# Causal attention in an eight-core transformer layer: both heads of a pair in one pass over the keys instead of one head after the other

## The chip, the cores and the metric

The kernel runs on all 8 cores of one Trainium2 chip (trn2). Each core computes one batch element and none talks to another. The metric is the device time in microseconds of the slowest core.

## The reference

One layer, post-norm, on x of shape (8, 2048, 1024), f32. The change touches the attention only.

```python
q = (x @ Wq + bq).reshape(b, s, 16, 64)      # k and v the same way
q = _apply_rope(q, sin, cos); k = _apply_rope(k, sin, cos)
scores = jnp.einsum('bqhd,bkhd->bhqk', q, k) * scale
scores = scores + jnp.where(causal, 0.0, -10000.0)
attn = jax.nn.softmax(scores, axis=-1)
ctx = jnp.einsum('bhqk,bkhd->bqhd', attn, v).reshape(b, s, 1024)
x = _layernorm(x + ctx @ Wo + bo)
# router: softmax, top 2 of 8 experts
# out = shared expert + sum over 8 experts of w[e] * expert(e), each computed densely
x = _layernorm(x + out)
```

## The kernel before

The program is written out by hand: every engine gets its instructions in the order of the code, and waits on semaphores are placed by `Ring` (buffers used in turn) and `Prog.wait`. VectorE (DVE), ScalarE (ACT) and GpSimd (POOL) also wait, before each operation, for their own previous one (`Prog.op`, `SELF_FENCE`).

The stages on a core are these. First x is transposed to xbf and v is computed for all heads. Then comes attention, which is the function shown below. Then the output projection with the layer norm and the router, then nine experts (the shared one and eight), each with 4096 hidden units, then the last layer norm. The experts' weights come as f32 and are converted to bf16 by DMAs from HBM to HBM (`precast_expert`: four DMAs of 4096 KB per expert). They are issued on POOL's queue, experts 0 and 1 at the start, expert j + 2 in attention pair j.

Attention works on 8 pairs of heads (j). For each pair:

- POOL issues the loads of wq and wk (256 KB each, two buffers each), then the conversion of expert j + 2. PE waits for both loads.
- PE projects q and k for both heads of the pair (L354, 64 matmuls, 128x128 weights), ACT moves them to SBUF with the bias (L363), PE permutes them (L372), DVE multiplies with the sine table (L379), POOL multiplies with the cosine table and adds (L388, L393). Head A stands on partitions 0 to 63 of qr_sb and kr_sb, head B on 64 to 127.
- Then, head after head, four windows of 512 queries. A window has 4, 8, 12 or 16 key tiles of 128 keys, since later keys are masked; the last four of a window carry the causal mask. For each key tile PE computes the scores into a buffer of pS (L467, or L455 and L460, where the mask is added by a matmul with the identity), ACT takes the exponential into et (L472), and one tile later PE adds the values (L405, into pCt) and the sum of the exponentials (L409, a matmul with a column of ones, into pSm). Two pS and three et buffers are in use.
- At the end of a window DVE copies the sums to SBUF (L488) and takes the reciprocal (L491, one partition, 512 elements). At the fourth key tile of the next window PE spreads it over 128 partitions (L419, f32, which runs as two matmul instructions), DVE copies that to SBUF (L425) and multiplies it with the values (L431).

The next pair's first operation on qr_sb waits for the scores of this pair, so the loads for pair j + 1 are issued on POOL right behind the rope of pair j.

Of the kernel before, what the change touches and what calls it, by code (L numbers as in the profile page):

```python
# [8 lines left out]
F32 = mybir.dt.float32  # L9
# [5 lines left out]
S = 2048  # L15
# [119 lines left out]
def build_nc():  # L135
# [20 lines left out]
    din("sel8", [8, 1024], BF16)  # L156
    y = nc.dram_tensor("y", [S, D], F32, kind="ExternalOutput").ap()
# [26 lines left out]
    sel8 = E(nc.sbuf_tensor("sel8_s", [8, 1024], BF16))  # L184

# [19 lines left out]
    for name, dst in (("identf", identf), ("ropec", ropec), ("ropes", ropes),  # L205
                      ("prm", prm), ("identb", identb), ("trit", trit),
                      ("bqr", bq_sb), ("bkr", bk_sb), ("bor", bo_sb),
                      ("br1r", br1_sb), ("br2", br2row), ("bv", bvrow),
                      ("sel8", sel8)):
        p.dma("sync", dst[:, :], d[name], dC)  # L210
# [91 lines left out]
    with ExitStack() as ph:  # L302
# [7 lines left out]
        et_sb = [ph.enter_context(nc.sbuf_tensor(f"et{i}", [128, 512], BF16)) for i in range(3)]  # L310
# [3 lines left out]
        pS = [ph.enter_context(nc.psum_tensor(f"pS{i}", [128, 512], F32)) for i in range(2)]  # L314
        pCt = [ph.enter_context(nc.psum_tensor(f"pCt{i}", [128, 512], F32)) for i in range(3)]
        pSm = [ph.enter_context(nc.psum_tensor(f"pSm{i}", [1, 512], F32)) for i in range(2)]
        pMs = ph.enter_context(nc.psum_tensor("pMs", [128, 512], F32))

        for eng in ("tensor", "scalar", "vector", "gpsimd"):
            p.wait(eng, dC, consts_d)  # L320

# [8 lines left out]
        pms_free = 0  # L330
        recip_free = 0
# [3 lines left out]
        for j in range(NCH):  # L335
# [61 lines left out]

            def emit_av(pa):
                p.wait("tensor", tA, pa["ex"])
                p.op("tensor",  # L400
                     lambda e, o=pa["ctslot"][pa["r0"]:pa["r0"] + 64, :],
                     l=vbuf[:, pa["kt"] * D + pa["h"] * 64: pa["kt"] * D + pa["h"] * 64 + 64],
                     r=pa["ets"][:, :], st=(pa["kt"] == 0), sp=(pa["kt"] == pa["nkt"] - 1),
                     tp=(0, pa["r0"]):
                     e.matmul(o, l, r, start=st, stop=sp, tile_position=tp))  # L405
                sm = p.op("tensor",
                          lambda e, o=pa["smslot"][:, :], r=pa["ets"][:, :],
                          st=(pa["kt"] == 0), sp=(pa["kt"] == pa["nkt"] - 1):
                          e.matmul(o, ones_b[:, :], r, start=st, stop=sp),  # L409
                          inc=tT)  # L410
                et_ring.release(pa["eti"], tT, sm)
                return sm

            def emit_norm(pn):
                nonlocal recip_free, pms_free
                p.wait("tensor", tV, pn["rc"])
                p.wait("tensor", tV, pms_free)
                bt = p.op("tensor", lambda e:
                          e.matmul(pMs[:, :], ones_f[:, :], recip_sb[0:1, :],  # L419
                                   start=True, stop=True), inc=tT)  # L420
                recip_free = bt
                rslot, rbi = rb_ring.acquire("vector")
                p.wait("vector", tT, bt)
                bv_ = p.op("vector", lambda e, o=rslot[:, :]:
                           e.tensor_copy(o, pMs[:, :]), inc=tV)  # L425
                pms_free = bv_
                r0_, j_, win0_ = pn["r0"], pn["j"], pn["win0"]
                cv = p.op("vector",
                          lambda e, o=ctx[r0_:r0_ + 64, j_ * S + win0_: j_ * S + win0_ + 512],
                          i=pn["ctslot"][r0_:r0_ + 64, :], r=rslot[r0_:r0_ + 64, :]:  # L430
# [6 lines left out]
            for hh in range(2):  # L437
                h = 2 * j + hh
                r0 = 64 * hh
                for qh in range(2):  # L440
                    for ws in range(2):
                        win0 = qh * 1024 + ws * 512
                        nkt = qh * 8 + ws * 4 + 4
                        ctslot, cti = ct_ring.acquire("tensor")
                        smslot, smi = sm_ring.acquire("tensor")
                        for kt in range(nkt):
                            sslot, ssi = ps_ring.acquire("tensor")
                            ets, eti = et_ring.acquire("scalar")
                            off = kt * 128 - win0
                            if off >= 0:  # L450
                                p.op("tensor",
                                     lambda e, o=sslot[:, :],
                                     l=kr_sb[r0:r0 + 64, kt * 128:(kt + 1) * 128],
                                     r=qr_sb[r0:r0 + 64, win0:win0 + 512]:
                                     e.matmul(o, l, r, start=True, stop=False))  # L455
                                scol = 384 - off
                                st_t = p.op("tensor",
                                            lambda e, o=sslot[:, :],
                                            m=trit[:, scol:scol + 512]:
                                            e.matmul(o, identb[:, :], m, start=False,  # L460
                                                     stop=True), inc=tT)
                            else:
                                st_t = p.op("tensor",
                                            lambda e, o=sslot[:, :],
                                            l=kr_sb[r0:r0 + 64, kt * 128:(kt + 1) * 128],
                                            r=qr_sb[r0:r0 + 64, win0:win0 + 512]:
                                            e.matmul(o, l, r, start=True, stop=True),  # L467
                                            inc=tT)
                            p.wait("scalar", tT, st_t)
                            ex = p.op("scalar",  # L470
                                      lambda e, o=ets[:, :], i=sslot[:, :]:
                                      e.activation(out=o, in_=i, func=AF.Exp,  # L472
                                                   bias=cst[:, 0:1], scale=cst[:, 1:2]),
                                      inc=tA)
                            ps_ring.release(ssi, tA, ex)
                            if kt == 3 and pend_norm is not None:
                                emit_norm(pend_norm)
                                pend_norm = None
                            if pend_av is not None:
                                emit_av(pend_av)  # L480
# [581 lines left out]
```

How the kernel before makes its waits and increments, by code:

```python
    def wait(self, eng, sem, val):  # L43
        if val <= 0:
            return
        if sem == self.SELF_FENCE.get(eng):
            if self._lastwait.get(eng, 0) >= val:
                return
            self._lastwait[eng] = val
        h = self.sems[sem]
        self.q[eng].append(lambda e, h=h, v=val: e.wait_ge(h, v))
# [1 line left out]
    def op(self, eng, build, inc=None, n=1):  # L53
        own = self.SELF_FENCE.get(eng)
        if own is not None:
            self.wait(eng, own, self.cnt[own])
            if inc is None:
                inc, n = own, 1
        if inc is None:
            self.q[eng].append(build)
            return None
        self.cnt[inc] += n
        h = self.sems[inc]
        self.q[eng].append(lambda e, b=build, h=h, k=n: b(e).then_inc(h, k))
        return self.cnt[inc]
# [1 line left out]
    def dma(self, eng, out, in_, sem):  # L67
        self.cnt[sem] += 16
        h = self.sems[sem]
        self.q[eng].append(lambda e, o=out, i=in_, h=h: e.dma_start(out=o, in_=i).then_inc(h, 16))
        return self.cnt[sem]
```

## Time and profile before

| | us |
|---|---|
| median of 3 runs | 6456.24 |
| all runs | 6455.94, 6456.24, 6901.99 |
| profiled execution | 6476.09 |
| its span, slowest core (3) | 6474.3 |
| spans of the 8 cores | 6447.9 to 6474.3 |
| attention stage in it (first projection to first load of the next stage) | 444.5 to 2064.6 |

The profile is that of core 3. Its spans are from the first to the last instruction; PE is TensorE's matmul, PEld its weight load, which can lie beside a matmul. PEclk is the clock that TensorE was granted, as a share of 2.4 GHz. The ends of matmuls are modelled and overlap the next one's start, so distances between starts are the better measure of what one costs.

### The profile page before, as it was taken

To read this page: it belongs to the slowest core of one execution; us is meant where nothing else is said; L and a number is where in the kernel's file an instruction comes from. 1 tells how busy PE (TensorE), PEld (TensorE's weight loads), DVE (VectorE), ACT (ScalarE), POOL (GpSimd) and SP (SyncE) were. 2 spreads that over 40 slices of the span, in tenths; PEclk is the share of its full clock that TensorE was granted. 3 is DMA by queue.
4 is the path that set the end of the run, shared out by engine and by line. 5 is a ranking of instruction groups with operands and counts; after the bars stand their busy time and mean duration, and the time that the engine had idled before them with its cause. 6 is when DMAs were issued, how large, how long until landed. Compare 5 with 4: busy or idle time off the path is not lost. (4 is left out here: it accounts for less than half of the span.)

```text
span 6474.3 us, 62496 instructions; the slowest of 8 cores (6447.9 to 6474.3 us)
## 1 busy us (share of the span) xinstructions
PE 5732.0 (89%) x22486; PEld 2264.1 (35%) x22486; DVE 987.7 (15%) x1255; ACT 1488.4 (23%) x2064; POOL 834.8 (13%) x717
## 2 busy tenths in 40 slices
PE   0069988899888589999999999999999999999996
PEld 0031111111111334444444444444444444444443
DVE  0012222222222401100100110111011001001104
ACT  0013333333333431122122112212211221221122
POOL 0010111101110000001211221121022012112211
PEclk9995555555555789999999999999999999999996
DMA  9949998788101110101010010101010010101101
GB/s 127 119 77 112 112 112 94 82 98 91 20 1 17 52 40 33 46 33 46 27 53 27 33 46 33 46 27 53 27 44 35 33 46 27 53 27 39 40 33 59
DMA packets 40060, 342.76 MB, mean 53 GB/s; under 512 B 5579, under 2 KB 5963, under 8 KB 16468
## 3 DMA queue, kind: packets, MB, share of 16 engines
q0 software_dynamic: 10368, 159.92, 21.7%
q1 hardware_dynamic: 29396, 178.85, 7.5%
q8 instruction: 191, 3.13, 0.2%
q14 instruction: 105, 0.86, 0.1%
HBM read 490.27 MB, written 159.38 MB: 100 GB/s over the span
## 5 line engine op out<-in xcount | busy, mean ns | idle before, releaser
L879 PE MATMUL pE<-h1bf,w2s 128*128 128x512 bf16 x9216 | 2010.4, 381 | 20.0 <-ACT h1bf L861 20.0
L850 PE MATMUL pE<-x2bf,w1s 128*128 128x512 bf16 x9216 | 2011.1, 381 | 6.9 <-DMA w1s<-w1bf 6.9
L861 ACT ACTIVATE h1bf<-pE,b_sb 128x512 bf16<-128x512 f32 x1152 | 791.7, 687 | 3155.7 <-PE pE L850 3155.5
L879 PEld LDWEIGHTS pE<-h1bf,w2s 128*128 128x128 bf16 x9216 | 904.7, 98 | 1125.6 <-issue 88.5
L850 PEld LDWEIGHTS pE<-x2bf,w1s 128*128 128x128 bf16 x9216 | 905.6, 98 | 1109.7 <-issue 35.4
L911 POOL TENSOR_TENSOR x<-x,tmp 128x512 f32<-128x512 f32 x512 | 647.9, 1266 | 3491.9 <-DVE tmp L902 3491.9
L472 ACT ACTIVATE et<-pS,cst 128x512 bf16<-128x512 f32 x640 | 497.7, 778 | 886.5 <-PE pS L460 455.3
L902 DVE SCALAR_TENSOR_TENSOR tmp<-pE,b_sb,wb 128x512 f32<-128x512 f32 x256 | 192.1, 751 | 1604.8 <-PE pE L879 1604.8
L405 PE MATMUL pCt<-et,vbuf 128*64 128x512 bf16 x640 | 401.9, 628 | 32.0 <-ACT et L472 32.0
L902 DVE SCALAR_TENSOR_TENSOR tmp<-pE,wb 128x512 f32<-128x512 f32 x256 | 177.0, 691 | 1620.5 <-PE pE L879 1620.5
L409 PE MATMUL pSm<-et,ones_b 128*1 128x512 bf16 x640 | 373.6, 584 | 0.0
L245 PE MATMUL pX<-identf_s,xstage 128*128 128x128 f32 x128 | 30.8, 423 | 342.4 <-DMA xstage<-x 341.0
L467 PE MATMUL pS<-qr_sb,kr_sb 64*128 64x512 bf16 x384 | 223.1, 606 | 0.0
L405 PEld LDWEIGHTS pCt<-et,vbuf 128*64 128x64 bf16 x640 | 81.4, 127 | 395.1 <-issue 395.1
L491 DVE RECIPROCAL recip_sb<-sums_sb 1x512 f32<-1x512 f32 x64 | 213.8, 3341 | 6.6
L455 PE MATMUL pS<-qr_sb,kr_sb 64*128 64x512 bf16 x256 | 154.2, 602 | 61.9 <-POOL kr_sb L393 61.9
L388 POOL TENSOR_TENSOR qr_sb<-q_sb,ropec_s 128x512 bf16<-128x512 bf16 x32 | 37.1, 1160 | 1225.9 <-ACT q_sb L363 1222.4
L488 DVE COPY sums_sb<-pSm 1x512 f32<-1x512 f32 x64 | 43.4, 679 | 873.1 <-PE pSm L409 872.1
L419 PE MATMUL pMs<-recip_sb,ones_f 1*128 1x512 f32 x128 | 132.2, 1134 | 36.4 <-DVE recip_sb L491 36.4
L460 PE MATMUL pS<-trit_s,identb_s 128*128 128x512 bf16 x256 | 155.9, 609 | 0.0
L409 PEld LDWEIGHTS pSm<-et,ones_b 128*1 128x1 bf16 x640 | 50.6, 79 | 279.3 <-issue 279.3
L245 PEld LDWEIGHTS pX<-identf_s,xstage 128*128 128x128 f32 x128 | 25.2, 223 | 347.5 <-issue 347.5
(121 smaller groups left out, 1400.0 us busy)
## 6 DMA issues: line engine op xcount, KB each, us to landing
w1bf<-w1r POOLq DMA_DIRECT2D x18, 4096.0 KB, 119.7
w2bf<-w2r POOLq DMA_DIRECT2D x18, 4096.0 KB, 154.6
w1s<-w1bf SPq DMA_DIRECT2D x72, 1024.0 KB, 7.2
w2s<-w2bf SPq DMA_DIRECT2D x72, 1024.0 KB, 7.7
xstage<-x SPq DMA_DIRECT2D x16, 512.0 KB, 4.4
xres<-x SPq DMA_DIRECT2D x16, 512.0 KB, 3.3
y<-ybuf SPq DMA_DIRECT2D x16, 512.0 KB, 2.6
wv_sb<-wv POOLq DMA_DIRECT2D x8, 256.0 KB, 16.3
```

The lines of the kernel that those rows point to most:

```text
L405: e.matmul(o, l, r, start=st, stop=sp, tile_position=tp))
L409: e.matmul(o, ones_b[:, :], r, start=st, stop=sp),
L455: e.matmul(o, l, r, start=True, stop=False))
L460: e.matmul(o, identb[:, :], m, start=False, stop=True), inc=tT)
L467: e.matmul(o, l, r, start=True, stop=True),
L472: e.activation(out=o, in_=i, func=AF.Exp, bias=cst[:, 0:1], scale=cst[:, 1:2]),
L491: rc = p.op("vector", lambda e: e.reciprocal(recip_sb[:, :], sums_sb[:, :]), inc=tV)
L850: e.matmul(o, l, r, start=st, stop=sp),
L861: e.activation(out=o, in_=i, func=AF.Silu, bias=b), inc=tA)
L879: e.matmul(o, l, r, start=st, stop=sp),
L902: e.scalar_tensor_tensor(o, i, b, w, ALU.add, ALU.mult),
L911: e.tensor_tensor(o, o, t, ALU.add), inc=tG)
```

## The change

Both heads of a pair are handled in the same pass over the key tiles. Per key tile PE computes the scores of head A and of head B into two pS buffers, ACT takes two exponentials, and one tile later PE does value A, value B, sum A, sum B. Head A's values go to the array's columns 0 to 63 and to partitions 0 to 63 of one pCt buffer, head B's to columns and partitions 64 to 127 (`tile_position`). The sums go to partitions 0 and 64 of one pSm buffer. The scores contract over rows 0 to 63 for A and 64 to 127 for B, as they did before. There are four windows per pair instead of eight, with twice the work in each.

The buffers change from two to four pS, from three to four et, and from three to two pCt; pMs goes, and pSm grows to 128 partitions. The copy to sums_sb goes: DVE takes two reciprocals, straight from pSm, on partitions 0 and 64. The broadcast is a matmul of a new constant sel2 (65 x 128) with recip_sb (65 x 512, set to 1 once), written into the same pSm buffer. ACT waits once per key tile, for the last of the score and mask matmuls, and signals once, after the second exponential.

```diff
-        et_sb = [... (f"et{i}", [128, 512], BF16)) for i in range(3)]
-        sums_sb = ph.enter_context(nc.sbuf_tensor("sums_sb", [1, 512], F32))
-        recip_sb = ph.enter_context(nc.sbuf_tensor("recip_sb", [1, 512], F32))
+        et_sb = [... (f"et{i}", [128, 512], BF16)) for i in range(4)]
+        recip_sb = ph.enter_context(nc.sbuf_tensor("recip_sb", [65, 512], F32))
-        pS = [... [128, 512] ... for i in range(2)]
-        pCt = [... [128, 512] ... for i in range(3)]
-        pSm = [... [1, 512] ... for i in range(2)]
-        pMs = ph.enter_context(nc.psum_tensor("pMs", [128, 512], F32))
+        pS = [... [128, 512] ... for i in range(4)]
+        pCt = [... [128, 512] ... for i in range(2)]
+        pSm = [... [128, 512] ... for i in range(2)]
...
             def emit_av(pa):
                 p.wait("tensor", tA, pa["ex"])
-                p.op("tensor", ... e.matmul(ctslot[r0:r0+64], vbuf[h], ets, tile_position=(0, r0)))
-                sm = p.op("tensor", ... e.matmul(smslot[:, :], ones_b, ets), inc=tT)
+                p.op("tensor", ... e.matmul(ctslot[0:64], vbuf[hA], etsA, tile_position=(0, 0)))
+                p.op("tensor", ... e.matmul(ctslot[64:128], vbuf[hB], etsB, tile_position=(0, 64)))
+                p.op("tensor", ... e.matmul(smslot[0:1], ones_b, etsA))
+                sm = p.op("tensor", ... e.matmul(smslot[64:65], ones_b, etsB, tile_position=(0, 64)), inc=tT)
...
             def emit_norm(pn):
-                bt = p.op("tensor", ... e.matmul(pMs[:, :], ones_f[:, :], recip_sb[0:1, :]), inc=tT)
+                bt = p.op("tensor", ... e.matmul(smslot, sel2[0:65, 0:128], recip_sb[0:65, :]), inc=tT)
...
-            for hh in range(2):
-                for qh in range(2):
-                    for ws in range(2):
+            for qh in range(2):
+                for ws in range(2):
...
+                        for (r0, sslot) in ((0, sslotA), (64, sslotB)):
+                            last = (off < 0) and (r0 == 64)
+                            p.op("tensor", ... e.matmul(sslot, kr_sb[r0:r0+64, kt], qr_sb[r0:r0+64, win0], stop=sp),
+                                 inc=(tT if last else None))
+                        if off >= 0:
+                            for sslot in (sslotA, sslotB):
+                                p.op("tensor", ... e.matmul(sslot, identb, trit[scol:scol+512], start=False, stop=True),
+                                     inc=(tT if sslot is sslotB else None))
+                        p.wait("scalar", tT, st_t)
+                        p.op("scalar", ... Exp, etsA <- sslotA)
+                        ex = p.op("scalar", ... Exp, etsB <- sslotB, inc=tA)
...
                     sm = emit_av(pend_av)
                     p.wait("vector", tT, sm)
-                        sc = p.op("vector", ... e.tensor_copy(sums_sb[:, :], smslot))
-                        rc = p.op("vector", ... e.reciprocal(recip_sb[:, :], sums_sb[:, :]), inc=tV)
+                    p.op("vector", ... e.reciprocal(recip_sb[0:1, :], smslot[0:1, :]), inc=tV)
+                    rc = p.op("vector", ... e.reciprocal(recip_sb[64:65, :], smslot[64:65, :]), inc=tV)
```

On PE, in the first window of pair 0 (all key tiles masked), the order before was this (pS score, pCt values, pSm sums; the number behind a name is its buffer):

```order
L455 MATMUL pS0<-qr_sb,kr_sb 128x512
L460 MATMUL pS0<-trit_s,identb_s 128x512
L455 MATMUL pS1<-qr_sb,kr_sb 128x512
L460 MATMUL pS1<-trit_s,identb_s 128x512
L405 MATMUL pCt0<-et0,vbuf 64x512
L409 MATMUL pSm0<-et0,ones_b 1x512
L455 MATMUL pS0<-qr_sb,kr_sb 128x512
L460 MATMUL pS0<-trit_s,identb_s 128x512
```

And in the same place now:

```order
L473 MATMUL pS0<-qr_sb,kr_sb 128x512
L473 MATMUL pS1<-qr_sb,kr_sb 128x512
L480 MATMUL pS0<-trit_s,identb_s 128x512
L480 MATMUL pS1<-trit_s,identb_s 128x512
L473 MATMUL pS2<-qr_sb,kr_sb 128x512
L473 MATMUL pS3<-qr_sb,kr_sb 128x512
L480 MATMUL pS2<-trit_s,identb_s 128x512
L480 MATMUL pS3<-trit_s,identb_s 128x512
L408 MATMUL pCt0<-et0,vbuf 64x512
L414 MATMUL pCt0<-et1,vbuf 64x512
L418 MATMUL pSm0<-et0,ones_b 1x512
L423 MATMUL pSm0<-et1,ones_b 1x512
```

Matmuls of one shape now stand in twos, the first for head A and the second for head B.

On PE, the passage from the first to the second window of a head, before, up to the broadcast of the reciprocal:

```order
L467 MATMUL pS0<-qr_sb,kr_sb 128x512
L467 MATMUL pS1<-qr_sb,kr_sb 128x512
L405 MATMUL pCt1<-et1,vbuf 64x512
L409 MATMUL pSm1<-et1,ones_b 1x512
L467 MATMUL pS0<-qr_sb,kr_sb 128x512
L405 MATMUL pCt1<-et2,vbuf 64x512
L409 MATMUL pSm1<-et2,ones_b 1x512
L467 MATMUL pS1<-qr_sb,kr_sb 128x512
L419 MATMUL pMs<-recip_sb,ones_f 128x512
```

And now:

```order
L408 MATMUL pCt1<-et2,vbuf 64x512
L414 MATMUL pCt1<-et3,vbuf 64x512
L418 MATMUL pSm1<-et2,ones_b 1x512
L423 MATMUL pSm1<-et3,ones_b 1x512
L473 MATMUL pS2<-qr_sb,kr_sb 128x512
L473 MATMUL pS3<-qr_sb,kr_sb 128x512
L434 MATMUL pSm0<-recip_sb,sel2_s 128x512
L408 MATMUL pCt1<-et0,vbuf 64x512
L414 MATMUL pCt1<-et1,vbuf 64x512
```

The broadcast still stands behind the fourth key tile's scores, and now writes the previous window's pSm buffer.

## Rows read from the trace of the kernel before

**Rows 1.** The page: the span in 40 slices, clock and DMA.
```profile
PEclk9995555555555789999999999999999999999996
DMA  9949998788101110101010010101010010101101
```

**Rows 2.** Stretches: length, PE busy and instructions, further engines where shown, clock, DMA share, GB/s.
```profile
677.50:849.00 171.50, 162.49 (x289) 0.50 1.01 113
...
850.00:880.00 30.00, 17.47 (x71) 6.85 (x69) 6.19 (x9) 5.50 (x8) 19.29 (x18) 0.84 0.98 108
```

**Rows 3.** Groups by line in the attention stage, 480 to 2064 us.
```profile
L472 ACT ACTIVATE et<-pS,cst 128x512 bf16<-128x512 f32 x638 | 496.1, 778 | 875.2 <-PE pS L460 444.1 <-PE pS L467 426.1 <-ACT et L472 0.7
...
L467 PE MATMUL pS<-qr_sb,kr_sb 64*128 64x512 bf16 x384 | 223.1, 606 | 0.0
L491 DVE RECIPROCAL recip_sb<-sums_sb 1x512 f32<-1x512 f32 x64 | 213.8, 3341 | 6.6
```

**Rows 4.** Timeline from 927 us: start us, length us, engine, line, operation.
```profile
927.49 0.61 PE L460 MATMUL pS<-trit_s,identb_s 128*128 128x512 bf16 x1
928.02 0.63 PE L405 MATMUL pCt<-et,vbuf 128*64 128x512 bf16 x1
...
930.22 1.03 PE L467 MATMUL pS<-qr_sb,kr_sb 64*128 64x512 bf16 x2
...
930.98 1.65 ACT L472 ACTIVATE et<-pS,cst 128x512 bf16<-128x512 f32 x2 [1.96 <-PE pS L467]
...
932.44 0.58 PE L409 MATMUL pSm<-et,ones_b 128*1 128x512 bf16 x1
932.96 0.60 PE L467 MATMUL pS<-qr_sb,kr_sb 64*128 64x512 bf16 x1
933.49 0.63 PE L405 MATMUL pCt<-et,vbuf 128*64 128x512 bf16 x1
...
934.05 0.58 PE L409 MATMUL pSm<-et,ones_b 128*1 128x512 bf16 x1
```

**Rows 5.** Timeline at the boundaries of pairs 1 and 2, and of 6 and 7.
```profile
842.58 0.68 DVE L488 COPY sums_sb<-pSm 1x512 f32<-1x512 f32 x1 [22.23 <-PE pSm L409]
...
846.95 2.04 PE L419 MATMUL pMs<-recip_sb,ones_f 1*128 1x512 f32 x2 [4.55 <-DVE recip_sb L491]
848.92 8.60 PE L354 MATMUL pS<-xbf,wq 128*128 128x512 bf16 x32
...
879.70 0.58 PE L455 MATMUL pS<-qr_sb,kr_sb 64*128 64x512 bf16 x1 [7.75 <-POOL kr_sb L393]
...
1859.34 1.03 PE L354 MATMUL pS<-xbf,wq 128*128 128x512 bf16 x2
```

**Rows 6.** Timeline: issues of wk by POOL; DMA issues: us to landing, last.
```profile
444.46 1.86 PE L354 MATMUL pS<-xbf,wq 128*128 128x512 bf16 x4 [9.49 <-DMA wk<-wkr]
...
476.48 0.55 POOL L70 DMA_DIRECT2D wk<-wkr  x1
...
wk<-wkr POOLq DMA_DIRECT2D x1, 256.0 KB, 122.9
...
678.13 0.55 POOL L70 DMA_DIRECT2D wk<-wkr  x1
...
wk<-wkr POOLq DMA_DIRECT2D x1, 256.0 KB, 77.7
...
879.79 0.55 POOL L70 DMA_DIRECT2D wk<-wkr  x1
...
wk<-wkr POOLq DMA_DIRECT2D x1, 256.0 KB, 31.4
...
wk<-wkr POOLq DMA_DIRECT2D x1, 256.0 KB, 7.1
```

**Rows 7.** Timeline: the first load of the stage behind attention.
```profile
2064.59 4.30 POOL L70 DMA_DIRECT2D wo_sb<-wor  x8 [173.73 <-POOLq L79]
```

**Rows 8.** Stretch behind the last conversion, columns as the second of rows 2.
```profile
1640.00:1660.00 20.00, 15.45 (x30) 3.62 (x30) 5.41 (x4) 3.58 (x5) 0.00 (x0) 0.50 0.00 0
```

More of the change, by code:

```diff
@@ L156, in build_nc @@
     din("sel8", [8, 1024], BF16)
+    din("sel2", [65, 128])
     y = nc.dram_tensor("y", [S, D], F32, kind="ExternalOutput").ap()
@@ L410, in emit_av @@
                           inc=tT)
-                et_ring.release(pa["eti"], tT, sm)
+                et_ring.release(pa["etiA"], tT, sm)
+                et_ring.release(pa["etiB"], tT, sm)
                 return sm
             def emit_norm(pn):
-                nonlocal recip_free, pms_free
+                nonlocal recip_busy
                 p.wait("tensor", tV, pn["rc"])
[L417 to L420, printed above, removed]
@@ L421, in emit_norm @@
-                recip_free = bt
+                bt = p.op("tensor", lambda e, o=pn["smslot"][:, :]:
+                          e.matmul(o, sel2[0:65, 0:128], recip_sb[0:65, :],
+                                   start=True, stop=True, skip_group_check=True),
+                          inc=tT)
+                recip_busy = bt
                 rslot, rbi = rb_ring.acquire("vector")
                 p.wait("vector", tT, bt)
-                bv_ = p.op("vector", lambda e, o=rslot[:, :]:
-                           e.tensor_copy(o, pMs[:, :]), inc=tV)
@@ L436, in build_nc @@
             pend_norm = None
-            for hh in range(2):
-                h = 2 * j + hh
-                r0 = 64 * hh
-                for qh in range(2):
-                    for ws in range(2):
[L442 to L450, printed above, removed]
-                                p.op("tensor",
[L452 to L480, printed above, removed]
-                            pend_av = dict(ex=ex, ctslot=ctslot, smslot=smslot,
-                                           kt=kt, nkt=nkt, ets=ets, eti=eti,
-                                           h=h, r0=r0)
-                        sm = emit_av(pend_av)
-                        pend_av = None
-                        p.wait("vector", tT, sm)
-                        sc = p.op("vector", lambda e, i=smslot[:, :]:
-                                  e.tensor_copy(sums_sb[:, :], i), inc=tV)
-                        sm_ring.release(smi, tV, sc)
-                        p.wait("vector", tT, recip_free)
-                        rc = p.op("vector", lambda e: e.reciprocal(recip_sb[:, :], sums_sb[:, :]),
-                                  inc=tV)
-                        pend_norm = dict(rc=rc, ctslot=ctslot, cti=cti,
-                                         r0=r0, j=j, win0=win0)
```

110 lines of the change are left out of this document (91 added, 19 removed).

## The prediction

> **What bounds the kernel now.** I read the page's forty slices first [rows 1]. Slices 3 to 12 are the attention stage: there the clock granted to PE reads 5 (half speed, the 1.2 GHz level) where the later stages read 9, and the DMA row is nearly full beside it. The change touches only this stage, 444.5 to 2064.6 us, so the rest of the span should stay as it is.
>
> Next, the stage by stretches [rows 2]: between 677.5 and 849 us PE is busy 162.5 of 171.5 us at clock 0.50, so PE ends the waits here. The DMA share in the same row is 1.01. The groups and the timeline [rows 3, 4] say what fills PE: matmuls that use half of the array's rows (64x128 scores), half of its columns (128x64 values) or one column (128x1 sums), and the full 128x128 mask. By [rows 3] ACT's exps are busy 496 of 1584 us, and DVE takes 64 reciprocals on one partition, 3.34 us each.
>
> The timeline [rows 4] gives the step that counts (durations overlap, so I take start to start): mask 0.53, value 0.56, sum 0.52, score 0.53 us. Two score matmuls of the same kind in a row last 1.03 together against 0.60 for one, so the second costs 0.43 (= 512 columns at 1.2 GHz); a matmul that follows one of another shape costs 0.10 more. One key tile of one head costs 1.61 us (value 0.56, sum 0.52, score 0.53), and 2.15 with the mask.
>
> Last, the boundary of two head pairs [rows 5] and the weight loads [rows 6]. A pair's pitch is (1859.34 - 848.92)/5 = 202.1 us. It checks: projections and rope 30.8 (848.92 to 879.70), 80 key tiles (48 x 1.61 + 32 x 2.15 = 146.1), 8 broadcasts of the reciprocal at 2.04 = 16.3, the wait for the last reciprocal 4.6: 197.8, and some 4 at the joins of the windows.
>
> **The queue behind the loads.** [Rows 6] decide the size of the gain. POOL issues a pair's wq and wk just after the rope of the pair before, behind a 16 MB conversion of expert weights. wk of pair 1 is issued at 476.48 and lands 122.9 later, at 599.4; of pair 2 at 678.13 + 77.7 = 755.8; of pair 3 at 879.79 + 31.4 = 911.2; of pair 4 in 7.1. Small loads of equal size do not take 122.9 and 7.1 by themselves: they wait in turn behind the conversions. Landings follow each other by 156.4 and 155.4, and the first (pair 0, 444.46, where PE waited for it) fits with 154.9; the mean is 155.6 us per expert. Now a pair takes 202, so the queue empties and nobody waits. A pair shorter than 155.6 will wait for its weights, each time.
>
> **The change part by part.**
>
> *Two heads in one pass.* The number of score, value, sum and mask matmuls stays the same. What changes is their order: always two of one shape in a row, on two disjoint halves of the array: score on rows 0 and 64, value on columns 0 and 64, sum the same. So of six changes of shape per key tile of a pair three remain, and eight become four with the mask.
>
> *The price x of the second matmul of such a two.* No row of before shows two different tiles one after the other. Upper bound: 0.43, the second of equal shape in [rows 4]. Lower bound: 0, if it runs beside the first; they share no cell, no PSUM partition (value, sum) or bank (scores), and read different operands. Below nothing is excluded, since the first one stands. I take x = 0, on the ground that none of the rows shows a common resource that is full, and keep 0.43. What makes this choice less bold: the result hardly depends on x until the pair's pitch exceeds 155.6 (below). The Trainium skill (TensorE: Matmul & The Clock Gate, Part 3) says that matmuls on different tiles run concurrently and gives 2.38x for three column tiles; no row here shows it. By that figure three matmuls cost 1.26 of one, an estimate of x = 0.13 x 0.43 = 0.06; with it the pair would cost 7 more and the kernel, which waits for its loads anyway, 6076.
>
> *With x = 0:* PE needs 1.61 per pair of unmasked tiles; with the mask 2.15 plus a second mask matmul of the same shape and weights, 0.43: 2.58.
>
> *ACT.* Two exps in a row take 1.65 [rows 4], 0.87 from start to start, so 1.74 per two. Scores go two tiles ahead (four pS). The loop is exp(k), then value and sum(k), then score(k+2), then exp(k+2): 1.65 + 1.61 + 0.35 for two hand-overs between engines ([rows 5]: copy at 842.58, 0.68 + 3.34 later 846.60, norm at 846.95), over two tiles: 1.8. With the mask PE's 2.58 is longer, so 2.6: 24 x 1.8 + 16 x 2.6 = 84.8.
>
> *Reciprocals.* Still 3.34 each, but two in a row (partitions 0 and 64) per window, 6.9 with the hand-over; from PSUM rather than SBUF, whose price no row shows: [rows 5] has DVE's copy out of PSUM at 0.68, and the SBUF reciprocal takes 3.34, so between none and +0.7 each; I take none. The copy into sums goes (0.68). In all 64 reciprocals as before, but PE's norm matmul at the fourth tile now meets a later one. PE has by then done 4 scores and 2 value-sum pairs, held back by exps; it reaches the norm some 4.5 us after the first exp, the reciprocals are ready about 6.4 after it. With the 2.04 of the norm, value, sum and score of the next tile behind it, ACT stands still for about 3.2. The join itself (value and sum, then score, after the last exp) is some 1.9: 5 x 3 joins = 15.
>
> *End of a pair.* Value and sum 1.1, two reciprocals 6.9, norm 2.04, hand-overs 0.3: 10.3, before the next projection. Norms: four of 2.04 instead of eight; K = 65 instead of 1, for which [rows 3, 4] show no dependence (score with 64 rows 0.606, mask with 128 rows 0.61).
>
> *Projection and rope*, 30.8: POOL's chain of 16 operations holds it (PE idles 7.75 for kr at its end [rows 5]). Four pS instead of two free PE earlier, nothing more. The new constant (33 KB), the memset of recip_sb and its wait come once: nothing.
>
> *Sum.* Pair: 30.8 + 84.8 + 15 + 10.3 = 140.9. That is below 155.6, so from pair 1 on PE waits for wk: 14.7 us per pair. Pair 7 starts at 444.46 + 7 x 155.6 = 1533.7. In before its projection starts at 1859.34 and the next stage's first load is issued at 2064.59 [rows 5, 7], 205.3 later; now 205.3 - (202.1 - 140.9) = 144.1 later, at 1677.8. The gain is 386.8. Had the loads not been in the way, it would be 8 x 61.2 = 490. The profiled execution is 6476.1 (span 6474.3): it becomes 6089; against the median, 6456.2, 6069.
>
> The conversions end at about 1534 instead of 1640 (behind it the DMA share is 0.00 [rows 8]), before the stage in which they are read; nothing collides there.
>
> **The clock.** In [rows 2] it is 0.50 while PE is busy 95%, and it is 0.84 in the projection between 850 and 880, where PE is less busy but the matmuls are full 128x128: what PE did before the clock fell was narrow matmuls. The two-head order lays two halves side by side, so it might rise. The Trainium skill (TensorE: Matmul & The Clock Gate, Part 1) says that a PE kept busy is given the full clock. By that rule, which gives rival 1, the clock of [rows 2] could not be 0.50; the trace contradicts it as far as busy time goes.
>
> **Rivals.**
> 1. *The clock rises inside attention.* For: full-width work has 0.84 and more. Against: exps leave PE idle in part. Then ACT sets all tiles: 40 x 1.74 = 69.6, joins 11, end of pair 8.7, rope 30.8: 120. The start of pair 7 stays; only 21 less at its end: 6048.
> 2. *The second matmul does not run beside the first* (x = 0.43). Then a pair costs per tile 3 x 0.97 = 2.9, with mask 3.86: 24 x 2.9 + 16 x 3.86 = 131.4, rope 30.8, norms inside 6.1, end 10 (reciprocals hidden inside): 178. Gain 8 x 24 = 193: 6263. The change would then not do its main work, only save changes of shape.
> 3. *Half of it*: rows pack, columns do not, or x about 0.3: pitch 158 to 165, PE-bound again, gain 8 x (202.1 - 161) = 329: 6127.
> 4. *Slower.* Alternating tiles drain PE fully: each matmul then costs its weight load and its own length, 0.10 + 0.61 = 0.71 [rows 3]: 24 x 6 x 0.71 + 16 x 8 x 0.71 = 193, with 47 for the rest 240: 8 x 38 = 304 slower, 6760. It turns at a mean step of (202.1 - 47)/272 = 0.57. Against: equal shapes follow each other at 0.43 today.
> 5. *No turn in the queue*: pairs start when ready, 490 gained, 5966. [Rows 6] speak against it.
>
> **How the numbers follow.** Forecast (packed, clock as now) 0.45; rival 1 0.32; rival 3 0.07; rival 2 0.10; rival 4 0.03; rival 5 0.03. The first two share the term that decides, 1533.7, and differ by what one pair costs, 120 to 155: 6048 to 6084, a few us more for the pitch (7 x 1). The range takes them and rival 3: 6030 to 6165. A measurement of this kernel tells about 2% from no change, 129 us; every case but the fourth gains more, so faster 0.95, same 0.02, slower 0.03.
>
> **What would show it.** Right: PE idle 10 to 35 us before the first wq matmul of pairs 1 to 7, released by the wk load; these starts 155.6 apart; second scores starting under 0.15 after the first; one DMA stretch at share 1.0 from 0.44 to 1.53 ms; PE waiting for recip_sb about 2 us in each window. Wrong: starts more than 156 apart with no wait for wk (packing fails, see the step from one half to the other), or wk landing early while conversions run.

## The result and the profile after

The changed kernel takes 6076.74 us (median of all its runs). In some executions of either kernel the cores of one die run at a lower granted clock, so times are compared from here on by the other executions alone: 6066.3 to 6083.4 us for the changed kernel, median 6071.5, and a ratio to the kernel before of 0.9406, 95% interval 0.9393 to 0.9419. The forecast was 6069, its range 6030 to 6165.

The profiled execution took 6068.34, its slowest core is core 0, span 6066.7 us. On that same core the next stage's first load, which ends attention, is issued at 1672.80, against 2075.13 on core 0 of before (2064.59 on core 3, [rows 7]). What follows that issue takes 4394 us on core 0, against 4387 before. So the gain lies in attention alone.

The page's forty slices, to be read against [rows 1]:

```profile
PE   0065566666656999999999999999999999999996
...
PEclk9996666666677999999999999999999999999997
DMA  9949999999021100100100101101001001001001
```

The stage has shrunk to slices 3 to 10. The clock there reads 6 instead of 5, PE is no longer full, and DMA is full to the end of slice 9. PE is not the bound any more. Who is, the waits of PE from 440 to 1690 us say (engine, tile and line, released by: us in total, times, longest):

```profile
PE pS L354 <- DMA wk<-wkr: 161.6, 8, 24.5
PE pCt L408 <- ACT et L491: 122.4, 183, 1.7
PE pSm L434 <- DVE recip_sb L511: 93.4, 32, 7.6
PE pS L473 <- POOL kr_sb L393: 91.1, 8, 11.6
```

The first line is the wait that the forecast named: eight waits, the first of 9.5 as in [rows 6], seven of 16 to 24.5. The timeline shows where they stand and how far apart (start, length, operation, idle time before it and its releaser):

```profile
447.10 9.65 PE L354 MATMUL pS<-xbf,wq 128*128 128x512 bf16 x32 [9.50 <-DMA wk<-wkr]
...
602.77 2.72 PE L354 MATMUL pS<-xbf,wq 128*128 128x512 bf16 x6 [21.12 <-DMA wk<-wkr]
...
758.50 6.67 PE L354 MATMUL pS<-xbf,wq 128*128 128x512 bf16 x20 [24.48 <-DMA wk<-wkr]
...
1536.42 9.42 PE L354 MATMUL pS<-xbf,wq 128*128 128x512 bf16 x32 [16.48 <-DMA wk<-wkr]
...
1672.80 2.71 POOL L70 DMA_DIRECT2D wo_sb<-wor  x5 [106.27 <-POOLq L79]
```

(1536.42 - 602.77)/6 = 155.6 us: the pitch of the landings in [rows 6], to a tenth; over the eight cores it is 155.1 to 155.8. wk of pair 1 is issued at 478.00 and lands 124.5 later, wk of pair 7 at 1416.35 and lands 119.8 later; in before the fourth and later ones took 7.1 or less, because the queue had run empty.

The key tiles look like this (start, length), at the beginning of pair 0:

```profile
481.33 0.61 PE L408 MATMUL pCt<-et,vbuf 128*64 128x512 bf16 x1 [0.44 <-ACT et L491]
481.33 0.63 PE L414 MATMUL pCt<-et,vbuf 128*64 128x512 bf16 x1
481.89 0.59 PE L418 MATMUL pSm<-et,ones_b 128*1 128x512 bf16 x1
481.90 0.59 PE L423 MATMUL pSm<-et,ones_b 128*1 128x512 bf16 x1
482.42 0.61 PE L473 MATMUL pS<-qr_sb,kr_sb 64*128 64x512 bf16 x2
482.96 1.04 PE L480 MATMUL pS<-trit_s,identb_s 128*128 128x512 bf16 x2
...
486.52 0.40 PE L408 MATMUL pCt<-et,vbuf 128*64 128x512 bf16 x1
486.52 0.40 PE L414 MATMUL pCt<-et,vbuf 128*64 128x512 bf16 x1
```

Value A and value B start at the same time, the sums 0.01 apart, and the two scores last 0.61 together, as long as one did. Only the masks, which share the whole array, follow each other (1.04). The steps from one shape to the next are those of before: 0.56, 0.52, 0.54. The Trainium skill (TensorE: Matmul & The Clock Gate, Part 3) gives about 4 ns between the starts of matmuls on different tiles; the trace, with 0.00 to 0.01 us, agrees. From 486.52 on the lengths are 0.40 instead of 0.61: here the clock is at its upper level, 2.4 GHz.

By stretches (columns as in [rows 2]), a whole pair with its wait:

```profile
602.00:757.00 155.00, 93.56 (x352) 24.38 (x352) 37.87 (x24) 67.69 (x88) 21.72 (x22) 0.65 1.00 112
```

The DMA share is 1.00 and PE is busy 94 of 155 us. [Rows 2] had 162.5 of 171.5 without the projection.

Inside a pair the clock goes up and down. Near the end of the second window of pair 1, where the key tiles carry the mask, it is at its upper level; behind it, at the lower one again (columns as above):

```profile
657.50:663.50 6.00, 4.53 (x26) 1.27 (x24) 0.31 (x1) 4.15 (x7) 0.00 (x0) 1.00 1.13 127
664.50:680.50 16.00, 13.19 (x42) 2.77 (x43) 6.77 (x4) 10.94 (x15) 0.00 (x0) 0.50 0.92 102
```

From score to score, over all eight pairs of core 0 and without the joins of the windows, an unmasked key tile of a pair takes 1.83 us and a masked one 2.19.

### The profile page after: what moved, and what is told of

Same layout as the page of the kernel before. It is cut to its first block and busy times, and to the rows that moved or that the text cites. A ratio compares the mean times of both kernels' runs of the same rounds, so it can differ in the third digit from the quotient of the medians.

```text
span 6066.7 us, 61212 instructions; the slowest of 8 cores (6054.4 to 6066.7 us)
## 1 busy us (share of the span) xinstructions
PE 5020.7 (83%) x22422; PEld 2146.7 (35%) x22422; DVE 901.4 (15%) x1128; ACT 1488.5 (25%) x2064; POOL 835.9 (14%) x717
## 5 line engine op out<-in xcount | busy, mean ns | idle before, releaser
L408 PE MATMUL pCt<-et,vbuf 128*64 128x512 bf16 x320 | 165.7, 518 | 124.4 <-ACT et L491 122.4
L473 PE MATMUL pS<-qr_sb,kr_sb 64*128 64x512 bf16 x640 | 162.8, 517 | 91.1 <-POOL kr_sb L393 91.1
L354 PE MATMUL pS<-xbf,wq 128*128 128x512 bf16 x256 | 75.8, 469 | 161.6 <-DMA wk<-wkr 161.6
L509 DVE RECIPROCAL recip_sb<-pSm 1x512 f32<-1x512 f32 x32 | 107.1, 3346 | 536.3 <-PE pSm L423 526.2
L414 PE MATMUL pCt<-et,vbuf 128*64 128x512 bf16 x320 | 171.7, 537 | 0.0
L423 PE MATMUL pSm<-et,ones_b 128*1 128x512 bf16 x320 | 159.0, 497 | 0.0
L418 PE MATMUL pSm<-et,ones_b 128*1 128x512 bf16 x320 | 158.4, 495 | 0.0
L408 PEld LDWEIGHTS pCt<-et,vbuf 128*64 128x64 bf16 x320 | 37.9, 119 | 306.6 <-issue 306.6
L434 PE MATMUL pSm<-recip_sb,sel_s 65*128 65x512 f32 x64 | 65.4, 1126 | 93.4 <-DVE recip_sb L511 93.4
```

Source lines behind the costliest of these rows:

```text
L408: e.matmul(o, l, r, start=st, stop=sp, tile_position=(0, 0), skip_group_check=True))
L414: e.matmul(o, l, r, start=st, stop=sp, tile_position=(0, 64), skip_group_check=True))
L418: st=first: e.matmul(o, ones_b[:, :], r, start=st, stop=False, skip_group_check=True))
L423: e.matmul(o, ones_b[:, :], r, start=st, stop=sp, tile_position=(0, 64), skip_group_check=True),
L473: e.matmul(o, l, r, start=True, stop=sp),
```

## The experiments

"Pitch" is the mean distance between the starts of pairs 1 to 7, on the slowest core unless cores are named. The runs were spread over several chips.

### Who sets the pace: weight loads ahead of the conversions

```diff
-        wq_sb = [... for i in range(2)]      # wk_sb the same
+        wq_sb = [... for i in range(8)]
-        for j in range(NCH):
-            wqs, wqi, qtok = wq_ring.load("gpsimd", ...)
-            wks, wki, ktok = wk_ring.load("gpsimd", ...)
+        for j in range(NCH):
+            wload.append(wq_ring.load("gpsimd", ...) + wk_ring.load("gpsimd", ...))
+        for j in range(NCH):
+            wqs, wqi, qtok, wks, wki, ktok = wload[j]
```

The same edit was made to the changed kernel and to the kernel before.

> The changed kernel, with eight wq and eight wk buffers and all sixteen loads issued ahead of the conversions of experts 2 to 8. Theory (the pairs wait for wk because it stands behind a conversion in POOL's queue): the waits of PE for wk, 161.6 us in the changed kernel, fall to the first one of some 10; pairs start 131 to 134 apart instead of 155.6; the kernel is 152 us faster than the changed one, 5915 to 5930. Rival (the conversions take the DMA engines' bandwidth, and whoever loads has to wait until they are done): no gain, 6060 to 6080, pitch 156.

Measured: 5937 to 5942 us, some 132 less than the changed kernel. PE waits for wk once, 8.7 us, at the first pair; pitch 133.1. The conversions still run at share 1.00, so it is the place in the queue and not the bandwidth that held the pairs. The gain is 20 short of what was expected, on which more below.

> The kernel before, with the same eight buffers and early loads. Theory: nothing waits for wk there, pitch 202, so no difference (within 8 us of before, ratio 0.999 to 1.001). Rival (early loads help in themselves): a gain like that of the loads in the changed kernel, 100 us or more.

Measured: 6456.5 to 6458.1, the kernel before 6457.0 to 6457.7 beside it. No difference. The queue only costs something once a pair is shorter than a conversion.

### Where the shorter pairs come from: the order on PE

First the twos were taken apart, the other parts of the change kept (score B and its mask stand behind value A and sum A). One more thing moved: the broadcast of the reciprocal now stands before the fourth key tile's scores instead of behind them.

```diff
-                        for (r0, sslot) in ((0, sslotA), (64, sslotB)):
-                            p.op("tensor", ... score)          # A, B
-                        ... mask A, mask B
-                            emit_av(pend_av)                   # value A, value B, sum A, sum B
+                        for (r0, sslot) in ((0, sslotA), (64, sslotB)):
+                            if r0 == 64 and pend_av is not None:
+                                emit_av_a(pend_av)             # value A, sum A
+                            p.op("tensor", ... score); ... mask
+                        ... exponentials
+                            emit_av_b(pend_av)                 # value B, sum B
```

> The changed kernel with all its buffers, two-head pass, half as many norms and signals, but PE's order is score A, (mask A), value A, sum A, score B, (mask B), value B, sum B, so that no two neighbours have one shape except at the start of a window. Theory (the gain comes from equal shapes on two tiles standing side by side): 24 x 3.22 + 16 x 4.3 = 146 for the key tiles, with 31 rope, 8 norms, some 11 for the end and the joins: pitch 195 to 198, clock 0.50, no wait for wk, 6400 to 6430, ratio to before 0.991 to 0.996. Rival (the gain comes from larger buffers, fewer norms and fewer hand-overs): pitch under 175, under 6250.

Measured: 6485.3 to 6485.9, slower than before by 28 us and 56 over the upper end of the expectation. Pitch 204.9, clock 0.50 in the key tiles. The timeline (start, length) tells why. The score here is score B, L499 is the exponential of head A and L503 that of head B:

```profile
704.00 0.61 PE L408 MATMUL pCt<-et,vbuf 128*64 128x512 bf16 x1 [1.53 <-ACT et L503]
...
705.05 0.60 PE L486 MATMUL pS<-qr_sb,kr_sb 64*128 64x512 bf16 x1
...
705.81 0.78 ACT L499 ACTIVATE et<-pS,cst 128x512 bf16<-128x512 f32 x1 [1.96 <-PE pS L486]
...
706.68 0.78 ACT L503 ACTIVATE et<-pS,cst 128x512 bf16<-128x512 f32 x1
...
707.60 0.60 PE L408 MATMUL pCt<-et,vbuf 128*64 128x512 bf16 x1 [0.33 <-ACT et L503]
```

A key tile of a pair takes 3.60, not 3.22. ACT waits for the second score before it starts the first exponential, and PE for the second exponential before value A: with score B late in the tile, value A, sum A, score B and both exponentials form a chain. That was a flaw of the experiment, and it was mended with a wait and a signal for each head:

```diff
-                        p.wait("scalar", tT, st_t)
-                        p.op("scalar", ... Exp, etsA)
+                        p.wait("scalar", tT, st_a)
+                        exa = p.op("scalar", ... Exp, etsA)
+                        p.wait("scalar", tT, st_t)
...
-                p.wait("tensor", tA, pa["ex"])                 # before value A
+                p.wait("tensor", tA, pa["exa"])
```

> As the run with the twos apart, but with one signal and one wait for each score and each exponential, since there ACT waited for both scores and PE for both exponentials (a key tile cost 3.60 instead of 3.22 us). Theory: PE then runs without these waits at the steps of the kernel before, pitch 195 to 198, clock 0.50, 6400 to 6430: five eighths of the key-tile matmuls' neighbours changed and the clock, nothing else, make the rest of the gain. Rival (the clock or the pass of two heads would gain on its own): under 6350.

Measured: 6375.4 to 6377.0, ratio 0.9876 (0.9858 to 0.9893), pitch 191.2: under the expectation by 23. The clock rose in parts of the windows even here (0.59 on the mean from 600 to 1300 us, with 0.50 in most stretches and 0.67 in some). So the two-head pass, larger buffers and half the norms, with that rise, are worth 11 us a pair, a sixth of the 69 to 71 that the change takes off a pair that waits for no load (202.1 before; 133.1 with early loads, 131.3 by itself below). The rest hangs on the twos. The place of the broadcast also differs between the two sides of this comparison; what that alone costs was not run.

Then the twos were kept, but the second was put on the first's tile. Head B's own scores are left out, and its values and sums land in head A's place:

```diff
-                                 l=kr_sb[r0:r0 + 64, ...], r=qr_sb[r0:r0 + 64, ...]
+                                 l=kr_sb[0:64, ...], r=qr_sb[0:64, ...]
...
+                c1 = 64 if first else 0
-                     lambda e, o=pa["ctslot"][64:128, :], ... tile_position=(0, 64)
+                     lambda e, o=pa["ctslot"][c1:c1 + 64, :], ... tile_position=(0, c1)
-                          lambda e, o=pa["smslot"][64:65, :], ... tile_position=(0, 64)
+                          lambda e, o=pa["smslot"][c1:c1 + 1, :], ... tile_position=(0, c1)
```

> The changed kernel with its order, but the second of each two uses the tile of the first: scores twice from partitions 0 to 63, values and sums of both heads into partitions 0 to 63 and 0 (except at the first key tile of a window, which stays as it is). So head B's scores are head A's, and value and sum of head B go to the wrong place. It costs as many matmuls and changes of shape as the changed kernel, without disjoint tiles. Theory (disjoint tiles run side by side, x = 0; on one tile x = 0.43): unmasked 2.9, masked 3.86 per key tile of a pair, pitch 172 to 180, clock 0.50 (the array is half used), no wait for wk, 6220 to 6275. Rival (neighbours of one shape are cheap on any tile): 6070 as the changed kernel.

Measured: 6080.3 to 6091.5, some 14 more than the changed kernel and 130 under the lower end of the expectation. This is the largest miss. The timeline has both halves of the answer:

```profile
717.60 0.63 PE L409 MATMUL pCt<-et,vbuf 128*64 128x512 bf16 x1
718.02 0.59 PE L415 MATMUL pCt<-et,vbuf 128*64 128x512 bf16 x1
718.55 0.38 PE L419 MATMUL pSm<-et,ones_b 128*1 128x512 bf16 x1
718.76 0.38 PE L424 MATMUL pSm<-et,ones_b 128*1 128x512 bf16 x1
...
719.61 0.39 PE L409 MATMUL pCt<-et,vbuf 128*64 128x512 bf16 x1
719.84 0.38 PE L415 MATMUL pCt<-et,vbuf 128*64 128x512 bf16 x1
```

On one tile the second does follow the first and not run beside it, 0.42 later at the lower level of the clock. But then the clock goes to its upper level, where the second costs 0.22. Over 600 to 1300 us the granted clock is 0.75 here, against 0.55 (0.50 in the key tiles) with the same number of matmuls and the same buffers in the first experiment's order, which changes shape each time. (Both scores of a two now also read the same operands; whether that touches the clock was not tried.) And what is still lost is hidden: PE waits 88.8 us for wk instead of 161.6, the pitch is 156.5 (155.2 to 156.5 over the cores).

To take the queue away, the same was run with early loads:

> Both seconds on the first's tile (same part left out and misplaced as in the earlier run on one tile), on top of the early loads, so that no pair waits for its weights. It measures what disjoint tiles are worth when the queue does not hide it. Theory (disjoint tiles save the second matmul; on one tile the clock rises more and gives most of it back; the queue hid the rest): pitch 143 to 146 instead of 133.2, 80 to 100 us slower than the early loads with disjoint tiles, 6020 to 6040. Rival (at the higher clock disjoint tiles are worth nothing): 5935 to 5950.

Measured: 6018.2 to 6023.1, pitch 146.2 (core 5; 146.2 to 146.7 on cores 4 to 7) against 133.1 beside disjoint tiles, clock 0.77 against 0.70. The disjoint tiles are worth 13 us a pair here, not 37 as at a fixed clock. Between the order that changes shape each time and twos on one tile lie 45 us a pair (191.2 against 146.2). A pair then has 136 changes of shape less (24 x 3 + 16 x 4), at 0.10 us ([rows 4]) some 14 us by estimate; the other 31 came with the clock, 0.77 instead of 0.59.

### What comes after the queue

The loads went three pairs ahead into four buffers, and wo into a buffer of its own during pair 4:

```diff
+        for j in range(3):
+            load_w(j)
         for j in range(NCH):
+            load_w(j + 3)
+            if j == 4:
+                for k in range(8):
+                    p.dma("gpsimd", wo_sb[...], d["wor"][k]..., dWo)
```

> The changed kernel with four wq and wk buffers, loads issued three pairs ahead, and wo loaded during pair 4 into a buffer of its own. Theory (the early loads gained 152 in the pairs, and lost 26 again because wo then stood behind the last conversions: PE waited 46.0 us for it instead of 20.0): no wait for wo, pitch 133, 5890 to 5905. Rival (the early loads' gain was cut by something else): 5930 to 5945.

Measured: 5937.4 to 5941.1, no different from the early loads: the theory on wo falls. wo was issued from 981.6 on and had landed by 1098, and still PE did not start. The waits of PE from 1480 to 1600 us:

```profile
PE pO L658 <- PEq L79: 44.2, 1, 44.2
```

L79 is the block that holds the attention instructions of all engines. What holds its end showed when the pairs were made shorter still:

```diff
-                        if kt == 3 and pend_norm is not None:
+                        if kt == 5 and pend_norm is not None:
...
+                if nm == "q" and pend_norm is not None:       # next pair, behind the q projection
+                    emit_norm(pend_norm)
```

> In addition, the norm of a window is issued at the sixth key tile of the next one instead of the fourth, and the last norm of a pair behind the q projection of the next. Theory (PE's 93.4 us of waits for recip_sb, 7.6 at each pair's end and 1.4 at three windows, and what ACT loses by them, go): pitch 121 to 125, 5810 to 5835. Rival (the reciprocals are hidden anyway, or DVE is late for rope): no gain over the run with loads ahead.

Measured: 5930.3 to 5932.8 and a pitch of 116.7, 16.5 less than without the late norms on the slowest cores and 14 less by the medians of the eight (118.3 against 132.6), which the total does not show. By stretches (us, length, the five engines' busy time, clock, DMA share, GB/s) and PE's waits:

```profile
1400.00:1450.00 50.00, 0.00 (x0) 0.00 (x0) 0.00 (x0) 0.00 (x0) 0.00 (x0) 0.50 1.03 113
...
1520.00:1540.00 20.00, 0.00 (x0) 0.00 (x0) 0.00 (x0) 0.00 (x0) 0.00 (x0) 0.50 1.00 111
1540.00:1550.00 10.00, 0.00 (x0) 0.00 (x0) 0.00 (x0) 0.00 (x0) 0.00 (x0) 0.50 0.28 52
1550.00:1570.00 20.00, 16.49 (x71) 7.02 (x71) 0.00 (x0) 6.78 (x9) 0.00 (x0) 0.83 0.09 27
```

```profile
PE pO L662 <- PEq L79: 162.6, 1, 162.6
```

All engines stand still from 1392 to 1552 while the last conversions run, and go on some 8 us after the last of their packets. No instruction of the program waits for them there. So the end of the block, where all engines meet, waits for the DMAs that POOL has issued; the next run tests it. Which part of leaving the block waits was not looked for. The same wait accounts for the 20 us that the early loads lacked: their pairs were done at 1516, wo was issued at 1543.5.

So two of the seven conversions were moved to the beginning of the experts' stage:

```diff
-            if j + 2 < NE:
+            if j + 2 < 7:
                 precast_expert(j + 2)
...
         h1_consumed = 0
+        precast_expert(7)
+        precast_expert(8)
```

> The run with loads ahead and late norms, and the conversions of experts 7 and 8 issued at the start of the experts' stage instead of in attention. Theory (that run did all its pairs by 1400 us, then PE stood 162.6 us because the attention block ends only when POOL's last conversion has landed, at 1541 to 1552; the same wait cut the early loads' gain): five conversions end by 1265, the block ends with the pairs at about 1400, pitch 117 as there, 5775 to 5800. Rival (something else between the stages takes that time, or the two conversions cost the experts as much later): 5900 to 5935.

Measured: three runs from 5894 to 5977. The block now ends with the pairs (projection at 1406.1 instead of 1552.7), as expected, and with it the rival that something else between the stages takes that time falls. But most of the gain is lost again in the experts' stage. PE's waits from 1600 to 2100 us:

```profile
PE pE L883 <- DMA w1s<-w1bf: 53.0, 5, 12.2
PE pE L912 <- DMA w2s<-w2bf: 46.1, 4, 12.5
```

Weight loads of the experts (1 MB each, hidden in before) come late while 4 MB conversions fill the engines, and the clock is lower there: 0.73 to 0.90 from 1600 to 2000 us. The runs differ more than elsewhere.

> The same with both seconds on the first's tile (same part left out and misplaced as in the earlier runs on one tile). Nothing in the queue hides anything now, so it gives the price of disjoint tiles alone. Theory: 13 us per pair, as between the two runs with early loads (146.2 against 133.1): 95 to 115 slower than the run beside it, 5875 to 5910. Rival (without the norms' waits PE is the bound and the tiles are worth the full 0.43 per second matmul): 200 or more slower.

Measured: 5978.4 to 5994.1. On the slowest cores the pitch is 131.0 against 118.0, 13 per pair as expected. The other cores say somewhat less: 126.4 to 131.6 against 117.5 to 118.8, by medians 128.4 against 118.4, so 10. The core with the highest clock (0.87 from 600 to 1300 us) has the shortest pitch of this run, the one with the lowest (0.83) the longest. Attention ends 85 later by medians of the cores, 97 on the slowest. The totals differ by less, about 60; with the other run's spread that difference says nothing. The price of disjoint tiles stands on the pitches: 10 to 13 us a pair.

> The changed kernel with nothing but the late norms (sixth key tile, last norm of a pair behind the next q projection). Between the runs with and without them, both with loads ahead, they shortened the pitch from 133.2 to 116.6. Theory (here the pitch is set by the queue in which wk stands): pitch stays 155.6 to 156, PE's wait for wk rises from 22 to 38 per pair, and only the last pair gains: 5 to 12 us faster than the changed kernel, 6060 to 6070. Rival (PE sets the pace of the changed kernel): 100 to 130 us faster.

Measured: 6079.5 to 6088.7, not faster than the changed kernel, rather 16 slower. The rival falls clearly. Here is PE's first wait, over the whole of core 1:

```profile
PE pS L356 <- DMA wk<-wkr: 287.0, 8, 43.9
```

What the late norms save goes into the wait for wk (161.6 before). The pitch is 157.0 to 158.5 on the cores of this chip, where the profile of the changed kernel has 155.1 to 155.8: conversions took 1 to 2% longer, and a kernel that waits for them follows. On the slowest cores seven pitches make 20 us of it (158.5 against 155.6), and the last pair, which no wait follows, is 5 shorter (129.1 from its start to PE's last matmul, against 134.0 in the changed kernel). That the chip and not the norms makes the conversions slower is likely but not shown: the late norms were not run on the other chip with the loads in the queue.

### A version that beats both

The two conversions were cut into 32 pieces of 1 MB, one issued with each weight load of experts 0 and 1:

```diff
+        def piece(e_i, n):                                     # behind each w1 and w2 load
+            if e_i < 2:
+                p.wait("gpsimd", tT, p.c(tT))
+                p.dma("gpsimd", dst, src, dPC[7 + e_i])
```

> As the run with two conversions later, but they are cut into 32 pieces of 1 MB, one for each weight load of experts 0 and 1, each issued when the step before is done. In that run the attention stage ended at about 1400 as expected, but PE then waited 99 us for the experts' weights (w1s, w2s) in nine waits while the two conversions ran at DMA share 1.0, and the experts' stage was some 130 longer. Theory (a weight load that meets 4 MB DMAs in the engines is late; pieces between the loads are not in its way): PE's waits for w1s and w2s under 20 us in all, 5780 to 5810. Rival (two conversions cost the same wherever they meet the experts' loads, or the memory itself is short): 5880 to 5930.

Measured: 5788.1 to 5791.4 in three runs, with 6458 to 6463 for the kernel before beside it: 0.896. (The interval over all comparable runs is wide, 0.8886 to 0.9008.) PE's only wait of note for expert weights from 1600 to 2600 us:

```profile
PE pE L888 <- DMA w1s<-w1bf: 6.2, 1, 6.2
```

The clock is back as well, and the DMA engines are no longer full. The stretch from 1800 to 1900 us, first in the run with the two conversions whole, then here:

```profile
1800.00:1900.00 100.00, 75.28 (x313) 32.31 (x314) 13.13 (x19) 0.00 (x0) 0.00 (x0) 0.82 1.02 129
1800.00:1900.00 100.00, 100.00 (x465) 45.30 (x463) 13.13 (x19) 13.76 (x20) 1.96 (x4) 1.00 0.32 84
```

The pieces are smaller and also spread over time, one in some 28 us. Which of the two helps was not separated. The kernel is 282 us faster than the changed one, with the same arithmetic.

## Why the prediction was right, and where not

*The queue.* The term that decides, pair 7 at 1533.7, was measured at 1536.4, on a core that starts 2.6 later; from the first projection it is 1089.2 forecast and 1089.3 measured. Read from three landings that nobody waited for in before, this term made the difference between 387 and 490 us. Early loads, which changed the order in the queue and the number of weight buffers it needs, took the wait away; in the kernel before they did nothing.

*x = 0.* Right: starts 0.00 to 0.01 apart. But the reason why it mattered little was only half of it. I had said the result hardly depends on x until the pitch passes 155.6, and rival 3 put x = 0.3 beyond that point. With x at its full value on every two the kernel took 6086, not the 6263 of rival 2.

*The clock.* This is the step that failed. The forecast took the clock as in before, 0.50 throughout the key tiles; rival 1 had it raised everywhere; it was 0.65 to 0.68 over the pairs, between the two. A pair by itself took 131.3 from its start to its last norm (602.77 to 758.50, less the wait of 24.5), against 140.9 forecast and 120 of rival 1. The term that is wrong in the sum is 16 x 2.6 for the masked key tiles: they took 2.19 on the mean, which is 6.6 of the 9.6 us, while the unmasked ones, where ACT sets the pace, took 1.83 against the 1.8 forecast. The other 3 us lie in the joins and the end of the pair and were not taken apart.

That the total is right all the same is owed to the queue, not to the pair: behind seven of the eight pairs PE waited for wk, which hid the error, and only the last one showed it. Attention took 1225.7 from its first projection, 7.6 less than forecast, and ended at 1672.8 instead of 1677.8. Where nothing waits in the queue, as with the early loads, each pair is shorter than forecast (pitch 133.1 against 140.9). The same step makes rival 2's price wrong by 180 us: I had priced a serial second matmul at the lower level of the clock, while with twos of equal shape it rises (0.76 and 0.77 on one tile). Its pair, measured without the queue, is 146.2 and not 178.

*What sets the clock* is shown only in part. From 600 to 1300 us, by medians of the cores (for the last but one, of cores 4 to 7):

| kernel | clock | PE busy |
|---|---|---|
| before | 0.56 | 88% |
| twos apart | 0.55 | 82% |
| twos apart, two signals | 0.59 | 85% |
| changed kernel | 0.68 | 61% |
| the same, late norms | 0.69 | 58% |
| early loads | 0.70 | 69% |
| loads ahead, late norms | 0.75 | 75% |
| twos on one tile | 0.76 | 73% |
| twos on one tile, early loads | 0.77 | 79% |
| twos on one tile, late norms, two conversions later | 0.85 | 80% |

All but the first have the same count of matmuls. The three orders (a change of shape each time, twos on two tiles, twos on one) do not overlap, and in like kernels the twos on one tile have 0.07 to 0.10 more than those on two. PE's busy share does not order these rows: it was 95% at 0.50 in [rows 2] and 60% at 0.65 in the pair shown above. The rule of the Trainium skill (TensorE: Matmul & The Clock Gate, Part 1), that a PE kept busy gets the full clock, does not describe these rows. Whether it is the work per matmul, the pauses at each change of shape or the share of the array that counts was not separated.

*The reciprocals.* From PSUM they took 3.35, so the lower bound was right. PE's wait for them inside windows is 1.4, and 7.6 at a pair's end, near the 7 assumed. Late norms took 14 to 17 us off a pair where nothing hid it, and nothing here.

*Two readings.* The forecast says that the DMA row is nearly full beside slices 3 to 12. In [rows 1] it is so in slices 3 to 9; the sum, which has the conversions end at 1640, uses it rightly. And the 0.10 that rival 4 takes for a weight load is not in [rows 3]; in the timeline of before these loads last 0.08 to 0.13.

*Rope.* 30.7 again (447.10 to 477.80). More pS buffers only lengthen PE's wait for POOL, from 7.75 to 11.2.

*"Nothing collides there."* True for the changed kernel, whose pairs end after the last conversion. It stops being true with the first improvement beyond it: the end of the block waits for the conversions.

*Rival 4* (a slower kernel through drained tiles) was wrong in its mechanism: steps between tiles are not dearer. The nearest to it was of my own making, a single signal for two heads in an order that puts the second late. Rival 5 falls with the pitch.

## What to carry to other kernels

Before you price a shorter compute stage, look at the landings of its loads, also of those that nobody waits for: issue time plus time to landing gives the pace of the queue in front of them, and that pace is the floor of the new stage as long as they stay in that order. Put small loads that compute needs ahead of bulk copies in the same queue, and keep bulk copies out of a block whose end all engines have to reach.

Matmuls that use half of the array's rows or columns should stand in twos of one shape, on disjoint halves where the data allow. Price each term at the clock that the new order will have, or at both levels: here some 31 us a pair came with the clock, by the estimate above, and 10 to 13 with the packing.

## What the runs showed of the hardware that was not expected

- The granted clock differs with the order of narrow matmuls, and PE's busy share does not order it: 0.55 to 0.59 with a change of shape each time at 82 to 88% busy, 0.68 to 0.75 with twos on two tiles at 58 to 75%, 0.76 to 0.85 with twos on one tile at 73 to 80%.
- The end of the block waited 162.6 us in one run for DMAs issued by POOL, although no instruction waits for them, and not at all when the last two conversions were issued later.
- HBM-to-HBM conversions, with the two loads between them, took 155.1 to 155.8 us per expert in the profile of the changed kernel and 157.0 to 158.5 in one on another chip; only a kernel that waits for them shows it.
- 1 MB weight loads that met 4 MB conversions came up to 12.5 us late on the slowest core; with 1 MB pieces issued between them, one wait of 6.2 was left.
